# The last program of a three-layer kernel in another order: earlier norms, a later second burst, queries sent from two queues

## The reference

```python
x = x + tanh(g_xattn[0]) * cross_attention(layernorm(x), ctx)     # 16 heads of 16, "stablemax"
x = x + tanh(g_ffn[0])   * moe(layernorm(x))                      # 64 experts, top 8, plus a shared feed-forward
x = x + tanh(g_xattn[1]) * softmax_attention(layernorm(x), ctx)   # 16 heads, no projections
x = x + tanh(g_ffn[1])   * butterfly_ffn(layernorm(x))            # 256 -> 1024 -> butterfly, gelu, butterfly -> 256
```

## Time and profile before

| | us |
|---|---|
| median of 3 runs | 1287.01 (1283.85 to 1287.62) |
| profiled execution, its own time | 1287.01 |
| span from first to last instruction | 1285.2 |
| TensorE busy | 1070.0 (83%) |
| VectorE busy | 797.2 (62%) |
| ScalarE busy | 737.6 (57%) |
| GpSimd busy | 356.7 (28%) |
| mean granted TensorE clock | 0.912 |

### The profile page before, as it was taken

How to read it: one execution, slowest core, us unless ns; L and a number is a source line. 1 busy time by engine, 2 the same in 40 slices (tenths; PEclk the granted TensorE clock), 3 DMA queues, 4 the chain that set the end, 5 groups by cost and what they waited for, 6 DMA issues and landing times.

```text
span 1285.2 us, 17761 instructions
## 1 busy us (share of the span) xinstructions
PE 1070.0 (83%) x5713; PEld 776.7 (60%) x5713; DVE 797.2 (62%) x1988; ACT 737.6 (57%) x1451; POOL 356.7 (28%) x313
## 2 busy tenths in 40 slices
PE   4788887789876789998899837869989989999988
PEld 2344454345444677876687626746766767677567
DVE  4578677877778654555654445476577666765443
ACT  1898898889854435665656320543455545444542
POOL 2000000000000005777777310104242533413223
PEclk8798898988877999999999967876999999999998
DMA  6455435443120316888887442120133131220000
GB/s 151 116 135 151 125 98 145 122 112 86 34 103 35 137 28 160 209 210 239 195 200 172 98 107 77 31 78 27 43 101 102 25 100 49 72 69 1 19 17 17
DMA packets 97404, 128.44 MB, mean 100 GB/s; under 512 B 26976, under 2 KB 69344, under 8 KB 97056
## 3 DMA queue, kind: packets, MB, share of 16 engines
q1 hardware_dynamic: 83312, 106.91, 28.9%
q0 software_dynamic: 12288, 18.88, 8.2%
q10 hardware_dynamic: 1712, 1.51, 0.6%
HBM read 66.15 MB, written 30.70 MB: 75 GB/s over the span
## 4 chain that ended last, share of the span: by engine, by line
PE 50%; DVE 21%; ACT 14%; issue 6%; SPq 3%; DMA 3%; POOL 1%; ACTq 1%; DVEq 0%; POOLq 0%
PE psum L1054 6%; PE psum L1039 5%; PE psum L881 5%; PE psum L897 4%; PE psum L788 3%; PE psum L957 3%; PE psum L916 3%; ACT weights L1114 3%; PE psum L764 3%; PE psum L966 3%; PE psum L986 2%; ACT weights L1110 2%; DVE stats L1317 2%; SPq L690 2%; PE psum L710 2%
## 5 line engine op out<-in xcount | busy, mean ns | idle before, releaser
L764 PE MATMUL psum<-q_stack,k_stack 96*128 96x512 f32 (+1 forms) x256 | 127.9, 525 | 40.8 <-DVE weights L1438 22.3
L1792 POOL TENSOR_SCALAR vareps<-moments 128x4 f32<-128x4 f32 x32 | 10.0, 314 | 533.5 <-DVE moments L1320 533.5
L1254 ACT ACTIVATE weights<-psum 128x512 f32<-128x512 f32 x160 | 94.1, 595 | 82.2 <-PE psum L764 73.5
L1438 DVE SCALAR_TENSOR_TENSOR weights<-psum,weights 128x512 f32<-128x512 f32 x160 | 102.8, 681 | 49.9 <-ACT weights L1118 49.7
L986 PE MATMUL psum<-k_stack,q_stack 96*128 96x256 f32 x256 | 89.8, 399 | 46.8 <-DVE peaks L1693 35.5
L1693 DVE TENSOR_REDUCE peaks<-psum 128x2 f32<-128x308 f32 x256 | 107.5, 469 | 18.4 <-PE psum L988 17.9
L1837 POOL TENSOR_TENSOR hidden<-hidden_whole,hidden 128x512 fp32r<-128x512 f32 x64 | 82.1, 1283 | 122.0 <-DVE hidden L1741 122.0
L1812 POOL DMA_INDIRECT expert_sums<-made,sum_rows x64 | 102.7, 1605 | 44.1 <-DVE made L1663 25.9
L881 PE MATMUL psum<-feat_parts,w_shared_up 128*128 128x512 f32 x384 | 102.9, 420 | 7.3 <-ACT shared_silu L1165 2.8
L1110 ACT ACTIVATE weights<-psum 128x512 f32<-128x512 f32 x160 | 88.9, 596 | 24.8 <-issue 13.9
L1054 PE MATMUL psum<-w_con_high,hidden 128*128 128x256 f32 x512 | 101.8, 297 | 0.0
(11 more groups left out here) (201 smaller groups left out, 2486.0 us busy)
## 6 DMA issues: line engine op xcount, KB each, us to landing
expert_w<-in_expert_w SPq DMA_DIRECT2D x64, 384.0 KB
q_stack<-q_stage SPq DMA_DIRECT2D x96, 128.0 KB, 2.4
q_stack<-q_stage SPq DMA_DIRECT2D x192, 64.0 KB, 2.0
expert_sums<-zeros SPq DMA_DIRECT2D x6, 1408.0 KB, 7.9
fetched<-expert_sums SPq DMA_DIRECT2D x16, 512.0 KB, 4.5
rows_scratch<-rows SPq DMA_DIRECT2D x8, 640.0 KB, 3.2
k_raw<-in_k SPq DMA_DIRECT2D x16, 300.0 KB
x<-in_x SPq DMA_DIRECT2D x8, 512.0 KB, 4.7
```

Source lines behind the costliest of these rows:

```text
L764: T.matmul(to, k[0:row, head_at(head), :], q[0:row, head // 2, :], start=True, stop=True).then_inc(scored, 1)
L1254: A.activation(weights1[n % 6][:, :], score_bank[n % 2], ACT.Exp).then_inc(exped, 1)
L1438: V.scalar_tensor_tensor(weights[n % 9][:, :], score_bank[n % 5], 1.0, weights[n % 9][:, :], ALU.add, ALU.max).then_inc(weighted, 1)
```

## The change

The order of the last program is changed, and one pair of sends moves to another queue. Nothing that is computed changes.

- Opening: the fetch and addition of half 1's expert sums stand ahead of half 0's query sends and three of the key splits, the values are loaded at once, and the shared feed-forward of halves 6 and 7 is dealt out among the peaks, so that it is finished before the first score.
- Half 0: `split_up` and `split_con` stand at steps 8 to 13, formerly 7 to 17.
- Every half: `norm f` and `bias_out` at step 3 (before 5 and 7), `turn_f` at 6 (before 8), `add_experts` at 5 (before 6), the second burst and its peak units at 14 (before 13), so `peaks` at 15 (before 14).
- The sends of the last two quarters of half 0's queries are issued by ScalarE.

```diff
--- before.py
+++ after.py
@@ -301,17 +301,15 @@
 
 
 
-PEAKS_AT = (-2, -1, 0, 1, 3, 4, 5, 6, 9, 9, 9, 9, 13, 13, 13, 13)
+PEAKS_AT = (-2, -1, 0, 1, 3, 4, 5, 6, 9, 9, 9, 9, 14, 14, 14, 14)
 
 PEAKS_SECOND = tuple(range(HT * PAIRS // 2))
 
-UP_AT, CON_AT, VALUES_AT = (7, 9, 12, 14), (16, 17), 8
-
-LATE_AT = (5, 9, 13)
+WEIGHTS_FROM = 8
 
 KEYS_AT = (10, 11, 13, 15)
 
-BURST_AT = (9, 13)
+BURST_AT = (9, 14)
 
 
 def peak_units(h, c):
@@ -339,7 +337,7 @@
         peak += peak_units(h + 2, c - PER_HALF)
         if c == 0:
             units.append(("fetch", h + 2))
-        if c == 6:
+        if c == 5:
             units += [("add_experts", h + 2, i) for i in range(SUMS)]
         if c == 10:
             units += norm_units("q1", h + 2)[:2]
@@ -363,11 +361,9 @@
     if 1 <= h <= HALVES:
         if c == 2:
             units += norm_units("f", h - 1)[:2]
-        if c == 5:
-            units.append(norm_units("f", h - 1)[2])
-        if c == 7:
-            units.append(("bias_out", h - 1))
-        if c == 8:
+        if c == 3:
+            units += [norm_units("f", h - 1)[2], ("bias_out", h - 1)]
+        if c == 6:
             units.append(("turn_f", h - 1))
         for b, at in enumerate(BURST_AT):
             if c == at:
@@ -378,29 +374,29 @@
 
 
 def plan_last():
-    plan = [("fetch", 0), ("load_k1", 0, 0), ("load_k1", 0, 1)]
+    plan = [("fetch", 0), ("load_k1", 0, 0), ("load_k1", 0, 1), ("load_v1", 0)]
     late = Stream(plan)
     for h in range(HALVES - LATE, HALVES):
         late.add(("shared", h), shared_steps(h))
     late.step()
-    plan += [("add_experts", 0, i) for i in range(SUMS)] + norm_units("q1", 0)[:2]
+    plan += [("add_experts", 0, i) for i in range(SUMS)]
+    plan += norm_units("q1", 0)[:2] + [("key_split1", 0, 0), ("load_k1", 0, 2)] + norm_units("q1", 0)[2:]
     late.step()
-    plan += [("key_split1", 0, 0), ("load_k1", 0, 2)] + norm_units("q1", 0)[2:]
+    plan += [("fetch", 1), ("turn_q1", 0)] + [("send_q1", 0, two) for two in range(PAIRS // 2)]
     plan += [("key_split1", 0, 1), ("load_k1", 0, 3)]
+    plan += [("add_experts", 1, i) for i in range(SUMS)]
     late.step()
-    plan += [("turn_q1", 0)] + [("send_q1", 0, two) for two in range(PAIRS // 2)]
+    plan += [("key_split1", 0, 2)]
     late.step()
-    plan += [("fetch", 1), ("load_v1", 0), ("key_split1", 0, 2), ("key_split1", 0, 3)]
-    plan += [("add_experts", 1, i) for i in range(SUMS)]
-    beside_peaks = {3: norm_units("q1", 1)[:2], 7: norm_units("q1", 1)[2:],
-                    9: [("turn_q1", 1)] + [("send_q1", 1, two) for two in range(PAIRS // 2)]}
+    plan += [("key_split1", 0, 3)]
+    beside_peaks = {1: norm_units("q1", 1)[:2], 3: norm_units("q1", 1)[2:], 5: [("turn_q1", 1)] + [("send_q1", 1, two) for two in range(PAIRS // 2)]}
     for n in range(HT * PAIRS // 2):
         plan.append(("peak", 0, n % HT, n // HT))
         plan += beside_peaks.pop(n, [])
-        if n in LATE_AT:
+        if n % 2 == 0:
             late.step()
     plan.append(("peaks", 0))
-    late.step()
+    late.step(2)
     plan.append(("scores1", 0))
     for n in range(20 * (HALVES + 1)):
         h, c = divmod(n, 20)
@@ -418,10 +414,12 @@
         if n % 5 == 2 and 5 < n <= len(CHUNKS) + 5:
             plan.append(("normalize1", (n // 5 - 1) // GROUPS, (n // 5 - 1) % GROUPS))
         if h == 0:
-            assert c < UP_AT[0] or not late.steps
-            plan += [("split_up", 2 * i) for i, at in enumerate(UP_AT) if c == at]
-            plan += [("split_con", 4 * i) for i, at in enumerate(CON_AT) if c == at]
-            if c == VALUES_AT:
+            assert c < WEIGHTS_FROM or not late.steps
+            if WEIGHTS_FROM <= c < WEIGHTS_FROM + 4:
+                plan.append(("split_up", 2 * (c - WEIGHTS_FROM)))
+            elif c in (WEIGHTS_FROM + 4, WEIGHTS_FROM + 5):
+                plan.append(("split_con", 4 * (c - WEIGHTS_FROM - 4)))
+            if c == WEIGHTS_FROM + 1:
                 plan += [("clear_v1", 1), ("load_v1", 1)]
         plan += beside(h, c)
     return plan
@@ -677,6 +675,9 @@
                 for part, row in parts:
                     engine.dma_start(st[row:row + 32, r::4, :], hi[32 * r:32 * r + 32, part, :, :]).then_inc(landed[r], 16)
 
+
+        SENT_BY_ACT = ((0, 2), (0, 3))
+
         def q1_sent(h):
 
             return 48 * (HALVES // 2) + 96 * (h // 2 + 1)
@@ -1240,6 +1241,10 @@
                 for c in range(CD):
                     evacuate(wide, ("turn_q1", h), q1_stage[:, 0, c, :], c).then_inc(queries_rounded, 1)
 
+            def send_q1(h, two):
+                if (h, two) in SENT_BY_ACT:
+                    send_pairs(A, h, two)
+
             def turn_peaks(h):
                 if h:
                     A.wait_ge(max_in[(h - 1) % 2], 64 * ((h - 1) // 2 + 1))
@@ -1297,7 +1302,7 @@
                      "sh_weights": sh_weights, "sh_split": sh_split_, "sh_up": sh_up, "sh_inner": sh_inner_,
                      "matrix": stage_matrix, "inside": inside, "across": across, "turn_up": turn_up,
                      "hots": hots, "turn": turn_got, "gate_up": gate_up, "key_split1": key_split1,
-                     "turn_q1": turn_q1, "peaks": turn_peaks, "exp1": exp1, "keep1": keep1,
+                     "turn_q1": turn_q1, "peaks": turn_peaks, "exp1": exp1, "keep1": keep1, "send_q1": send_q1,
                      "split_up": split_up, "split_con": split_con, "turn_f": turn_f, "up": up}
             for n, plan in enumerate((first, experts, last)):
                 if n:
@@ -1980,6 +1985,8 @@
                     S.dma_start(to[32 * j:32 * j + REST, 1, j::4, 0:HD], rest[:, :, j, :]).then_inc(v1_in[b % 2], 16)
 
             def send_q1(h, two):
+                if (h, two) in SENT_BY_ACT:
+                    return
                 if h >= 2:
                     S.wait_ge(scored, FIRST + PER_HALF * (h - 2) + 5 * (two + 1))
                 send_pairs(S, h, two)
```

## The result

The changed kernel took 1306.39 us (median of 4, 1304.27 to 1307.55), the one before 1287.32 (median of 4); the ratio is 1.0152 (95% interval 1.013 to 1.0175). Forecast: 1307. Timed again in a later session it was 1308.03 against 1284.09, ratio 1.0187 (1.0153 to 1.0221). So it is slower by 1.5 to 1.9%, 19 to 24 us.

A forecast was written before the change was run, and what follows sets the result against it. A steady half was taken to be bound by TensorE's work plus its few waits. The terms -17 + 0.5 + 32.5 - 0.6 + 4.7 gave +20 on 1287.01: forecast 1307 us, range 1298 to 1318.

The forecast's parts named there:

- The opening and half 0: Last program's start: the 15.94 us wait goes, first score 4.7 later, next steps shorter; -17, plus 0.5 for weight splits.
- The norm: Halves 2 to 6: norm ahead of step 3's reduces makes TensorE stand 3.9 us; 6.5 a half, +32.5 us.
- the clock's: Halves 2 to 6: after the 3.9 us wait TensorE runs at 1.2 GHz until the next burst; 4.8 us more each.
- the late bank: Step 4, halves 2 to 6: second matmul pair gets its bank 3.0 us later, less 1.3 for two swallowed waits.
- Rival (a): Halves 2 to 6: the clock stays up, so each costs 2.5 us; 1287 us in all; chance 0.12.
- The burst: Six half boundaries: peaks transposed in step 15, so TensorE waits 0.8 us more at each; +4.7 us.
- Half 1: Clock already low; step 4's second pair comes 2.0 us later, the 1.74 us wait at step 6 goes; 0.
- Half 7 and the tail: Half 7: the earlier turn fills the 2.00 us wait, -0.6 us; the tail behind its last score keeps its order.
- (b): Steady halves hide the norm's wait, given 3 us of VectorE slack in step 2; 1272 us; chance 0.16.
- (c): Opening gains little: first scores at 815 to 817, first term -5; 1319 us; chance 0.14.

The follow-up runs named there:

- the run with the norm back: The changed kernel with norm, bias and turn of the finished half back in steps 5, 7 and 8, expert sums in step 6; 1276.82 us, ratio 0.9937.
- the run with 32 repeats: The changed kernel, with TensorE repeating a matmul of step 4's peak unit 32 times into the bank it already holds; 1288.09 us, ratio 1.004.
- burst back: The changed kernel with only the second burst and the peaks beside it back in steps 13 and 14; 1292.48 us, ratio 1.0051.
- growing waits: The kernel before, with VectorE repeating a reduce of step 3 2, 4, 6, 8 and 10 times in halves 2 to 6; 1310.19 us, one run.
- the run with the norm in step 4: The kernel before with the new opening, norm and bias in step 4 and the turn in step 6; 1281.44 us, ratio 0.9984.
- experiment 2: The changed kernel with a TensorE matmul of step 4 repeated to fill its wait: 16 times 1297.16 us, 32 times 1288.09 us.

## Why the prediction was right

**The opening and half 0: -16.5 predicted, -16.1 (first pair) and -13.6 (second) measured.** Fetch at +11.75 us from the start (10.6 predicted), ScalarE's sends 8.2 us (10), first unit +31.9 (32.6), first score +74.8 (75.1), step 5's weigh +80.6 (81.6), the wait of 5.01 now 3.54. Two errors met: the sends were shorter, but behind them came the silu and 4.7 us of sh_up, not the key splits. In four of the nine profiles with 12 sends on ScalarE the clock fell once more ahead of the first score (the second of the changed kernel is one), and the score came at 77.6 to 77.8; in the other five it came at 74.6 to 75.6.

**The norm: +6.5 a half predicted, 5.7 and 6.3 measured (means of halves 2 to 6, against the run with the norm back).** The mechanism held to the digit: VectorE's idle 1.61 us (1.6), TensorE's wait 3.92 (3.9).

The mis-sized term is the clock's, "I let TensorE run at the low level from there to the next burst", 4.8 us. In half 2 of the first execution the low stretch did last to the burst, and there the sum fits: 10.98 us from the second pair to the first up matmul (924.35 to 935.33, predicted 11.0), and the half 6.8 us over the run with the norm back. In most halves the clock came back after 6.8 us, before the burst, and they grew by 5.3 to 5.5. The clock's price was 2.75 us a half in the first execution and 3.35 in the second.

The rest, the late bank, cost 2.9 to 3.0 us net with the clock up, and not the 3.0 - 1.3 of the sum. In the run with 32 repeats the waits of 0.57 and 0.45 that half 3 had with the norm back are gone, as predicted, but one for the turn's feature split stands in their place:

```profile
976.80 0.39 PE L992 MATMUL psum<-k_stack,q_stack 96*128 96x256 f32 x1 [0.89 <-DVE feats L1743]
```

Rival (a) had this wait (0.8) and came to 2.5 a half; the forecast's sum left it out. So a clock term that was too large and a bank term that was too small met, and how long the clock stays low changed from execution to execution (6.8 to 13.7 us behind the same wait): that the sum came within a microsecond of the first time is partly luck. The run with 32 repeats made rival (a) real: 1288.09 us, where (a) said 1287; against the kernel before in its session that is 4 us more, where (a) had none.

**The burst: +0.8 a half predicted, 0.8 to 1.1 measured (0.1 in half 4),** with its wait of 1.13 us for the peaks' landing (1.51 in the last).

**Half 1: 0 predicted; -3.0 in the first pair and +0.6 in the second measured.** It got the 3.9 us wait too, and lost another, whose cause I had not seen. VectorE, GpSimd and TensorE of half 1 in the kernel before, second profile:

```profile
868.32 5.50 DVE L1358 TENSOR_SCALAR normed<-x,moments,rstd 128x256 f32<-128x256 f32 x4
```

```profile
868.18 4.83 POOL L1827 TENSOR_TENSOR x<-x,fetched 128x1024 f32<-128x1024 f32 x2
```

```profile
874.26 0.58 PE L986 MATMUL psum<-k_stack,q_stack 96*128 96x256 f32 x1 [4.71 <-DVE peaks L1693]
```

The wait of 1.74 us at step 6 that I had counted as gone is the same thing in the first profile, where the norm took 4.70 us beside the same additions. Norming in step 3, the changed kernel is ahead of them, and its norm takes 1.38 us.

**Half 7 and the tail: -0.6 and a last boundary of 0.8 predicted; +0.6 in the first pair, -1.2 in the second.** The wait of 2.00 went, and one of 1.82 for the norm took its place.

**The sum:** 20 predicted; the last program grew by 15.2 and 21.9, and the timed difference was 19 and 24. Rivals (b) and (c) fell: no slack on VectorE in step 2, and a first score at +75 and +78, not at +85.

## What to carry to other kernels

Ahead of moving a step forward on an engine, look at what its neighbours hid: the four reduces between statistics and norm covered another engine's answer exactly. Without them the 1.6 us for that answer and the 1.4 us of the norm itself both came ahead of the reduce that TensorE needed: 3.0 us more standing. Price such a wait in two parts, the late work and the clock, and test them apart with work that changes nothing. And take the parts of a change separately: here one part was worth some 14 us, another cost 6, the third 21 alone and 28 to 32 beside the second, and the sum hid all three.

## What the runs showed of the hardware

- The granted clock fell to 0.50 at each of the 19 waits of 2.96 us or more in halves 2 to 6 (changed kernel twice, burst back, growing waits), mostly while TensorE still stood (up to 2.5 us before it resumed) and at the latest 0.6 us behind it. It did not fall at 1.94 (one case). At waits of 2.0 with the repeats ahead of them, and a wait of 1.1 some 12 us earlier, it fell in four halves of five. In the run with the norm in step 4 it fell in two halves of five, at waits of 0.91, 1.27 and 0.89 us within 6 us in one and of 0.91 and 1.27 alone in the other; three halves with the same waits saw no fall. The Trainium skill ("TensorE: Matmul & The Clock Gate", "A second HAM failure mode: psum-queue depth-cycling") says that frequent short idle spells between matmul groups, too, make the clock swing; those two halves agree.
- A stretch at 1.2 GHz cost 0.34 to 0.39 us for each us in this kernel, where work of TensorE alone would lose half by the two clock levels (halves of experiment 2).
- The same wait of 3.9 us was followed by low stretches between 3.4 us (burst back, halves 4 and 6) and 13.7 us (the changed kernel's second profile, half 4). What sets their length stays open.
- VectorE's norm took 5.3 to 5.6 us where GpSimd's two additions to x ran beside all of it, 3.4 and 4.7 where they caught a part, and 1.38 otherwise; the attention's x<-att took 1.94 instead of 0.48. The Trainium skill ("Trainium Architecture — The Big Picture", "What this means for kernel authors") names the port pair that VectorE and GpSimd share as the only one of SBUF's engine side that contends, with an exclusive lock; the rows agree, and where the norm stood ahead of the additions (changed kernel, norm in step 4) it took 1.38, though no run took the additions away.
- A query send took 0.67 us on SyncE while ScalarE issued its own at 0.68, and 0.63 when SyncE sent all 24: two queues did nearly halve the time (15.15 us to 8.2). The 12 key sends at the start had taken ScalarE 1.02 each.
